# Rebuilding the landmark stage of a four-stage transformer kernel: band matrices by transfer, landmark sums as products, scaling on ScalarE, projections by halves

## The chip, the core and the metric

The kernel runs on one core of one Trainium2 chip. The metric is the device time of one execution in microseconds (us), the median of several executions. TensorE, VectorE (DVE in the rows), ScalarE (ACT), GpSimd (POOL) and SyncE (SP, which issues transfers) run at the same time and wait for each other through semaphores.

## What is computed

The input x is 8 batches of 512 tokens with 256 features. Four layers follow one another: a Nyström attention A, a mixture of experts, an attention B, the experts again. Only attention A and the work ahead of it are touched:

```python
qkv = x @ w_qkv                      # x is layer-normalised; 16 heads of 64
q_l = q.reshape(b, H, M, l, DH).sum(axis=3) / l      # 64 landmarks of 8 tokens each
k_l = k.reshape(b, H, M, l, DH).sum(axis=3) / l
attn1 = softmax(q @ k_l.T); attn2 = softmax(q_l @ k_l.T); attn3 = softmax(q_l @ k.T)
attn2_inv = moore_penrose_inverse(attn2)   # starts from attn2.T / (max col sum * max row sum), over all batches
out = attn1 @ attn2_inv @ (attn3 @ v)
out = out + conv(out)                # 13 taps along the tokens, one set for each head
x = x + out.reshape(...) @ w_fc + b_fc
```

The maximum of the row and column sums is taken over all heads of all batches. So the inverse of the first batch can't begin before `attn2` of the last batch is known, and that is why a stage of its own, `landmarks`, stands ahead of `layer_a`.

## The kernel before

`landmarks` (from L154) works in these steps.

- SP issues the taps and a shifted identity, then the eight batches of x, 512 KB each, then the weights that `layer_a` needs (`la.load`). ACT's queue issues the query and key weights `wqk` (2 MB).
- In a loop of two rounds of four batches, VectorE takes the statistics of a batch (L290, L294), GpSimd makes 1/deviation (L269, L271), VectorE normalises (L300), TensorE transposes in eight products against the identity (L363), and VectorE sums groups of eight tokens out of the bank (L308) into `xsum`.
- When all eight batches are in `xsum`, TensorE makes 16 projections of two products each with 512 columns (L375), eight for `ql`, eight for `kl`; ScalarE scales each out of its bank (L247).
- `build_bands` (L447 to L454) makes the band matrices of the convolution, [128 x 140] for each head, four heads (a quarter) at a time: for each of 13 taps a product with a shifted identity and an addition. VectorE makes two quarters (`BANDS_DVE`) behind its part of the loop, GpSimd one. The fourth is made by GpSimd at the start of `layer_a`.
- Then the softmax of `attn2` over a batch (`sim`, 16 products of 64 columns, L387): VectorE maximum and shift (L325, L327), ScalarE exponential (L252), VectorE sum and reciprocal (L331, L333), GpSimd scaling (L277), TensorE transposition (`aT`, L397), ScalarE copy (L256), VectorE sums of both (L338, L343). At the end the maximum over partitions (L281) and its reciprocal (L350).
- SP stores `ql`, `kl`, `a` and `aT` of every batch to DRAM, 256 KB each, since the loop of `layer_a` loads them batch by batch. It waits for all of these stores at the end of the stage, and a barrier between the stages waits for every engine.

`layer_a` (from L468) begins with a prologue: SP loads the first `a` and `aT`, the value weights into `v_a` (1 MB), and the landmarks of the first batch into the block-diagonal `kl_diag` and `ql_diag`. GpSimd and VectorE zero four block-diagonal tensors. VectorE takes the statistics of batch 0 a second time (L601), GpSimd makes the deviation (L756), VectorE normalises (L613). The value weights are split into two parts, `wv_a_hi` on ScalarE (L872) and `wv_a_lo` on VectorE (L748). GpSimd then builds the fourth quarter of the bands while the loop over the batches runs. A batch begins on TensorE with its transposition (L1004); the products for `u` and `g` (L1012) and the values (L891) come behind. The inverse's steps (L950, L982) are interleaved in an order written out in the code.

The order on every engine is the order of the code; there is no planner. `Fills` gives each use of a PSUM bank its semaphore counts.

## Time and profile before

| | |
|---|---|
| median of 3 executions | 2665.5 us (2656.21 to 2667.6) |
| the profiled execution | 2670.99 us |
| its span in the trace | 2669.2 us |
| TensorE busy | 2247.3 us, 84% of the span |
| VectorE, ScalarE, GpSimd busy | 59%, 38%, 28% |
| mean granted TensorE clock | 0.928 |
| first eight batches' landmarks and the prologue of `layer_a` | 0 to 162.3 us |
| loop of `layer_a` | 162.3 to 1115 us |

The profiled execution takes 1.8 us more than its span. Busy shares are means over stages with different limits. What the change is worth is read from the stretch from 0 to about 290 us, where the stage and the first batch of `layer_a` lie.

### The profile page before, as it was taken

What the parts mean: (1) busy time and instruction counts of PE and PEld (TensorE: products, weight loads), DVE (VectorE), ACT (ScalarE), POOL (GpSimd) and SP (SyncE); (2) the same over time, 40 slices, a digit from 0 to 9 for tenths busy, and PEclk for the clock granted to TensorE, in tenths of its full rate; (3) what the DMA queues carried; (4) which work ended last, traced back from release to release, by engine and by line L of the source; (5) the groups of instructions that cost most, each with busy time, mean ns of one, the idle gap of its engine ahead of it and who ended that gap; (6) DMA issues with size and microseconds to landing.
All of it is one profiled execution on the core that took longest, in us unless ns stands there. A gap on an engine that the chain in (4) does not pass through costs nothing. (4 is left out here: it accounts for less than half of the span.)

```text
span 2669.2 us, 49971 instructions
## 1 busy us (share of the span) xinstructions
PE 2247.3 (84%) x18702; PEld 1776.6 (67%) x18702; DVE 1565.0 (59%) x3407; ACT 1013.9 (38%) x1828; POOL 759.2 (28%) x816
## 2 busy tenths in 40 slices
PE   4469999999999999699859993788888876895998
PEld 2357888788877888577749981445444445774997
DVE  7965547464554646378745653655555526874664
ACT  0223333333333333243424441345454553342553
POOL 4360101010110101136622233333333204662222
PEclk9779999999999999889979996899999998997999
DMA  4320000000000000212345536544444407112553
GB/s 148 99 68 10 10 9 17 2 17 10 9 10 9 11 8 2 78 56 80 127 151 141 140 57 149 91 73 73 74 73 73 73 27 230 40 44 64 139 143 56
DMA packets 152489, 179.60 MB, mean 67 GB/s; under 512 B 48761, under 2 KB 138769, under 8 KB 149137
## 3 DMA queue, kind: packets, MB, share of 16 engines
q1 hardware_dynamic: 137884, 155.67, 21.9%
q0 software_dynamic: 13440, 17.90, 4.1%
q8 instruction: 164, 2.69, 0.4%
q10 hardware_dynamic: 944, 2.88, 0.4%
q14 instruction: 57, 0.46, 0.1%
HBM read 107.66 MB, written 68.75 MB: 66 GB/s over the span
## 5 line engine op out<-in xcount | busy, mean ns | idle before, releaser
L2249 DVE TENSOR_REDUCE b_neg_max<-bank 128x1 f32<-128x512 f32 (+2 forms) x384 | 178.7, 506 | 184.4 <-PE bank L2477 182.1
L2369 ACT ACTIVATE b_probsT<-bank 128x512 f32<-128x512 f32 x320 | 185.9, 604 | 209.8 <-PE bank L2477 198.5
L2008 PE MATMUL bank<-e_hT_hi,k_rwkv 128*128 128x512 f32 x576 | 206.9, 401 | 2.9 <-DVE e_hT_lo L1912 2.9
L1933 DVE TENSOR_TENSOR e_square<-e_relu 128x512 f32<-128x512 f32 x144 | 99.7, 693 | 148.5 <-ACT e_relu L1972 146.1
L774 POOL TENSOR_TENSOR probs<-probs,rcp 128x512 f32<-128x512 f32 x64 | 66.7, 1044 | 382.8 <-DVE rcp L642 382.8
L1972 ACT ACTIVATE e_relu<-bank,k_bias 128x512 f32<-128x512 f32 x144 | 99.1, 688 | 199.4 <-PE bank L2008 199.2
L2021 PE MATMUL bank<-v_rwkv_hi,e_hidden_lo 128*128 (+1 forms) x576 | 162.5, 282 | 0.0
L2021 PE MATMUL bank<-v_rwkv_lo,e_hidden_hi 128*128 (+1 forms) x576 | 162.1, 282 | 0.0
L2021 PE MATMUL bank<-v_rwkv_hi,e_hidden_hi 128*128 (+1 forms) x576 | 161.8, 281 | 0.0
L621 DVE TENSOR_TENSOR conv_lo<-bank,conv_hi 128x512 fp32r<-128x512 f32 x64 | 44.2, 691 | 141.9 <-ACT conv_hi L791 141.9
L2477 PE MATMUL bank<-b_k_stacked,b_q_stacked 96*128 96x512 bf16 (+3 forms) x512 | 126.4, 309 | 0.0
L2008 PEld LDWEIGHTS bank<-e_hT_hi,k_rwkv 128*128 128x128 f32 x576 | 110.0, 191 | 22.3 <-DVE e_hT_lo L1912 3.7
L2477 PE MATMUL bank<-b_q_stacked,b_k_stacked 99*128 99x512 bf16 (+3 forms) x512 | 122.7, 302 | 0.0
L950 PEld LDWEIGHTS bank<-pi_t,wz 64*64 64x64 f32 x3072 | 98.5, 135 | 33.9 <-issue 31.4
L950 PE MATMUL bank<-pi_t,wz 64*64 64x64 f32 x3072 | 111.8, 222 | 5.0 <-DVE pi_t L689 5.0
L2008 PE MATMUL bank<-e_hT_lo,k_rwkv 128*128 128x512 f32 x288 | 114.5, 398 | 0.0
L756 POOL TENSOR_SCALAR a_rstd<-a_mv 128x4 f32<-128x4 f32 x8 | 1.8, 230 | 392.5 <-DVE a_mv L605 381.5
L2021 PEld LDWEIGHTS bank<-v_rwkv_hi,e_hidden_hi 128*128 128x128 f32 x576 | 108.4, 188 | 6.6
L2021 PEld LDWEIGHTS bank<-v_rwkv_lo,e_hidden_hi 128*128 128x128 f32 x576 | 108.6, 188 | 6.0
L1935 DVE TENSOR_TENSOR e_hidden_lo<-e_square,e_hidden_hi 128x512 fp32r<-128x512 f32 x144 | 99.6, 692 | 15.5 <-DVE e_square L1933 0.5
L2021 PEld LDWEIGHTS bank<-v_rwkv_hi,e_hidden_lo 128*128 128x128 f32 x576 | 108.2, 188 | 0.0
L1950 POOL DMA_INDIRECT scratch_x_out<-e_y,e_token x36 | 58.5, 1625 | 172.2 <-DVE e_y L1921 164.0
(358 smaller groups left out, 6431.9 us busy)
## 6 DMA issues: line engine op xcount, KB each, us to landing
k_rwkv<-scratch_k SPq DMA_DIRECT2D x16, 2048.0 KB, 7.4
scratch_b_parts<-b_part SPq DMA_DIRECT2D x96, 128.0 KB, 1.8
b_q_stacked<-scratch_b_parts SPq DMA_DIRECT2D x96, 128.0 KB, 4.5
b_k_stacked<-scratch_b_parts SPq DMA_DIRECT2D x96, 128.0 KB, 4.4
scratch_rows<-f_hq SPq DMA_DIRECT2D x18, 516.0 KB, 8.6
e_rows<-scratch_rows SPq DMA_DIRECT2D x18, 516.0 KB, 8.4
x_tokens<-in_x_dram SPq DMA_DIRECT2D x8, 512.0 KB, 7.7
scratch_x_out<-x_tokens SPq DMA_DIRECT2D x8, 512.0 KB, 3.0
```

Of the source, the lines that this page charges most:

```text
L621: nc.vector.tensor_tensor(lo, fills.data(*name)[:], hi.bitcast(F32), ALU.subtract).then_inc(fills.released(*name), 1)
L774: nc.gpsimd.tensor_tensor(probs, probs, spread(rcp1[:, f], NP), ALU.mult).then_inc(s["probs1_done"], 1)
L950: last = nc.tensor.matmul(data[h, j * M:(j + 1) * M], lhs[h, j], rhs[h, j], start=True, stop=True)
L1933: nc.vector.tensor_tensor(sq[:, q % 2], r[:, q % 2], r[:, q % 2], ALU.mult).then_inc(s["square_done"], 1)
L1935: nc.vector.tensor_tensor(h2[1][:, q % SQ_RING], sq[:, q % 2], h2[0][:, q % SQ_RING].bitcast(F32), ALU.subtract).then_inc(s["hidden_done"], 1)
L1950: nc.gpsimd.indirect_dma_start(x_out[:, :], bass.IndirectOffsetOnAxis(token[:, i % 3, t:t + 1], 0), y[:, i % 2, t, :], None, compute_op=AL ...
L1972: nc.scalar.activation(r[:, q % 2], fl.data("h", q)[:], ACT.Relu, bias=ff.k_bias[i % 2][:, c:c + 1]).then_inc(fl.released("h", q), 1)
L2008: last = nc.tensor.matmul(data[:], ff.k_part(i % 2, a)[:, k, c * P:(c + 1) * P], hT[b][:, i % 2, k], start=n == 0, stop=n == len(steps) - 1)
L2021: last = nc.tensor.matmul(fl.data("e", i, t // 2)[:, t % 2 * C:(t % 2 + 1) * C], h2[a][:, q % SQ_RING, t * P:(t + 1) * P], values[b], star ...
L2249: last = nc.vector.tensor_reduce(neg_max[:, half % 2, t, head + e:head + e + 1], data[:, at:at + (t + 1) * P], AX_X, ALU.max, negate=True)
L2369: nc.scalar.activation(probsT[:, ring, u], fl.data("st", pair, u)[:], ACT.Exp, scale=DB ** -0.5).then_inc(fl.released("st", pair, u), 1)
L2477: last = nc.tensor.matmul(data[:, at:at + size], weights[:, tile:tile + P], moving[:, first:first + size], start=False, stop=True, skip_gr ...
```

## The change

- **Bands.** The band matrices are laid out in the arrays that the kernel is given (`bands`), and come in by one transfer of 1.1 MB with 8960 bytes for each partition. GpSimd adds the centre diagonal in one operation of 2240 columns. `build_bands` is gone from both stages.
- **Landmark sums.** In place of transposing a batch and summing on VectorE, TensorE multiplies the normalised batch with a [128 x 16] matrix of ones (`lm_pool`): eight products of 16 columns (`pool`, L404), and ScalarE copies the sums out of the bank (`take_sums`).
- **Normalising.** ScalarE does it, with scale 1/deviation and bias -mean/deviation; GpSimd makes both in four small steps (`deviation`). Batch 0 is normalised into the tensor that `layer_a` reads, and isn't normalised again there.
- **Halves.** The projections are made for four batches at a time: 8 units of four products with 256 columns for each half. `pool` of batches 4 to 7 stands between those of the first half, `sim` and `aT` of batches 0 to 3 between those of the second.
- **Prologue.** The splitting of the value weights, the zeroing, the multiples of the identity, the fourth quarter and the loads of batch 0 move from `layer_a` into `landmarks`. The value weights land in `v_a`, and `aT` of batches 4 to 7 is later written over them.
- **Row sums.** The sum of the scaled rows is the row sum times its reciprocal, on 8 columns, and not a second reduction over 512.
- The loop of `layer_a` and the three other layers are as before.

```diff
+                load_x(0)
+                sp.dma_start(pool16[:], dram["pool"]).then_inc(consts_loaded, 16)
+                sp.dma_start(la.i64[:], dram["i64"]).then_inc(consts_loaded, 16)
+                for b in range(1, BATCHES_H):
+                    load_x(b)
+                sp.dma_start(wqk[:], dram["w_qkv"][:, 0:2 * INNER].rearrange("(k p) n -> p k n", p=P)).then_inc(w_loaded, 16)
+                for b in range(BATCHES_H, B):
+                    load_x(b)
+                sp.dma_start(wv_raw.rearrange("p (k n) -> p k n", k=CT), dram["w_qkv"][:, 2 * INNER:].rearrange("(k p) n -> p k n", p=P)).then_inc(
+                    wv_loaded, 16)
+                la.load(sp, dram)
                 sp.dma_start(core.ident[:], dram["ident"]).then_inc(core.ident_loaded, 16)
...
+                store_landmarks(0)
+                store_a(0)
+                store_landmarks(1)
+                sp.wait_ge(s["zeroed"], ZEROED)
+                sp.wait_ge(stored_first, 64)
+                la.load_a(sp, 0)
+                la.load_landmarks(sp, 0)
+                for b in range(1, B):
+                    store_a(b)
...
+                def centre(b):
+                    act.wait_ge(s["norm_steps"], (b + 1) * NORM_STEPS)
+                    if b >= 3:
+                        act.wait_ge(*full("pool", b - 2))
+                    for t in range(TT):
+                        nc.scalar.activation(xn_of(b)[:, t, :], cols(x, b * XB + t * C, C), ACT.Identity, bias=nmr[:, b, t:t + 1],
+                                             scale=rstd[:, b, t:t + 1]).then_inc(s["xn_done"], 1)
+                def take_sums(b):
+                    act.wait_ge(*full("pool", b))
+                    nc.scalar.activation(xsum[:, :, b * M:(b + 1) * M], fl.data("pool", b)[:, 0:CT * M].rearrange("p (k m) -> p k m", k=CT),
+                                         ACT.Copy).then_inc(fl.released("pool", b), 1)
...
+                for b in range(BATCHES_H):
+                    centre(b)
+                    if b:
+                        take_sums(b - 1)
+                take_sums(BATCHES_H - 1)
+                for i in range(PROJ):
+                    project(0, i)
+                    if i % 2 == 0:
+                        if i:
+                            take_sums(BATCHES_H + i // 2 - 1)
+                        centre(BATCHES_H + i // 2)
+                take_sums(B - 1)
+                act.wait_ge(wv_loaded, 16)
+                nc.scalar.activation(la.wv[0][:].rearrange("p k n -> p (k n)"), wv_raw, ACT.Copy).then_inc(s["wv_hi"], 1)
+                for i in range(PROJ):
+                    project(1, i)
+                    if i % 2:
+                        exponentials(i // 2)
+                        if i >= 5:
+                            take_turned((i - 5) // 2)
...
-                for n, q in enumerate(range(BANDS_DVE, BANDS_EARLY)):
-                    la.build_bands(nc.gpsimd, pool, n, q, pool_term, pool_signals)
...
+                def deviation(b):
+                    pool.wait_ge(s["mv_done"], (b + 1) * TT)
+                    g.tensor_scalar(var[:, b], mv[:, b, :, 1], EPS, None, ALU.add).then_inc(s["norm_steps"], 1)
+                    g.tensor_tensor(rstd[:, b], var[:, b], core.neg_half[:], ALU.pow).then_inc(s["norm_steps"], 1)
+                    g.tensor_tensor(nm[:, b], mv[:, b, :, 0], rstd[:, b], ALU.mult).then_inc(s["norm_steps"], 1)
+                    g.tensor_scalar(nmr[:, b], nm[:, b], -1.0, None, ALU.mult).then_inc(s["norm_steps"], 1)
+                    deviation(b)
+                pool.wait_ge(consts_loaded, CONSTS)
+                for tile, n in ((la.i7, 7.0), (la.i15, 15.0), (la.i13, 13.0 / 4)):
+                    g.tensor_scalar(tile[:], la.i64[:].unsqueeze(1).to_broadcast([P, GP, M]), n, None, ALU.mult).then_inc(s["eyes_done"], 1)
+                pool.wait_ge(la.loaded, la.loads)
+                g.tensor_tensor(la.band[:], la.band[:], la.centre[:].unsqueeze(1).to_broadcast([P, HA, BAND]), ALU.add).then_inc(s["centred"], 1)
...
-                for q in range(BANDS_DVE):
-                    la.build_bands(nc.vector, dve, q, q, dve_term, dve_signals)
...
+                dve.wait_ge(s["wv_hi"], 1)
+                flat = [w[:].rearrange("p k n -> p (k n)") for w in la.wv]
+                v.tensor_tensor(flat[1], wv_raw, flat[0].bitcast(F32), ALU.subtract).then_inc(s["wv_lo"], 1)
+                for b in range(B + 5):
...
+                        v.tensor_tensor(sums[:, 0, c], row_sum[:, c], row_rcp[:, c], ALU.mult).then_inc(s["rows_summed"], 1)
...
+                def pool(b):
+                    pe.wait_ge(s["xn_done"], (b + 1) * TT)
+                    pe.wait_ge(*free("pool", b))
+                    for t in range(TT):
                         for ct in range(CT):
...
+                            at = ct * M + t * (P // LG)
+                            last = nc.tensor.matmul(fl.data("pool", b)[:, at:at + P // LG], xn_of(b)[:, t, ct * P:(ct + 1) * P], pool16[:],
+                                                    start=True, stop=True)
+                    last.then_inc(fl.filled("pool", b), 1)
+                def proj(half, i):
+                    if i == 0:
+                        for b in range(half * BATCHES_H, (half + 1) * BATCHES_H):
+                            pe.wait_ge(*read("pool", b))
+                        pe.wait_ge(w_loaded, 16)
+                    pe.wait_ge(*free("proj", half, i))
+                    for q in range(2):
+                        n = 2 * i + q
+                        for ct in range(CT):
+                            last = nc.tensor.matmul(fl.data("proj", half, i)[:, q * LANDMARKS_H:(q + 1) * LANDMARKS_H],
+                                                    wqk[:, ct, n * P:(n + 1) * P], xsum[:, ct, half * LANDMARKS_H:(half + 1) * LANDMARKS_H],
+                                                    start=ct == 0, stop=ct == CT - 1)
+                    last.then_inc(fl.filled("proj", half, i), 1)
...
+                pe.wait_ge(consts_loaded, CONSTS)
+                for b in range(BATCHES_H):
+                    pool(b)
+                for i in range(PROJ):
+                    proj(0, i)
+                    if i % 2:
+                        pool(BATCHES_H + i // 2)
+                sim(0)
+                for i in range(PROJ):
+                    proj(1, i)
+                    if i in (4, 6):
+                        turn((i - 4) // 2)
+                    if i in (1, 3, 5):
+                        sim((i + 1) // 2)
+                for b in range(4, B):
+                    sim(b)
+                    turn(b - 2)
+                turn(B - 2)
+                turn(B - 1)
...
-    def build_bands(self, ops, eng, n, q, term, signals):
...
-        for k in range(1, TAPS):
-            eng.wait_ge(band_done, n * BAND_STEPS + k)
-            ops.tensor_tensor(term[:], tap(k), diagonal(k), ALU.mult).then_inc(term_done, 1)
-            eng.wait_ge(term_done, n * (TAPS - 1) + k)
-            ops.tensor_tensor(band, band, term[:], ALU.add).then_inc(band_done, 1)
-        eng.wait_ge(band_done, n * BAND_STEPS + TAPS)
-        ops.tensor_tensor(band, band, diagonal(PAD), ALU.add).then_inc(band_done, 1)
-        eng.wait_ge(band_done, (n + 1) * BAND_STEPS)
...
+                (self.band, dram["bands"].rearrange("p (h n) -> p h n", h=HA)), (self.centre, dram["band_centre"]),
...
-                for diag in (kl_diag, ql_diag):
-                    nc.vector.memset(diag[:], 0.0).then_inc(s["diag_zeroed"], 1)
-                for tile, n in ((i7, 7.0), (i15, 15.0), (i13, 13.0 / 4)):
-                    nc.vector.tensor_scalar(tile[:], la.i64[:].unsqueeze(1).to_broadcast([P, GP, M]), n, None, ALU.mult).then_inc(
-                        s["eyes_done"], 1)
-                dve.wait_ge(s["eyes_done"], 3)
-                statistics(0)
-                normalise(0)
-                dve.wait_ge(s["wv_hi"], 1)
-                flat = [w[:].rearrange("p k n -> p (k n)") for w in wv]
-                nc.vector.tensor_tensor(flat[1], wv_raw, flat[0].bitcast(F32), ALU.subtract).then_inc(s["wv_lo"], 1)
+                dve.sem_inc(s["stats_done"], TT)
+                dve.sem_inc(s["mv_done"], TT)
+                dve.sem_inc(s["xn_done"], TT)
...
-                for diag in (p_diag, avT_diag):
-                    nc.gpsimd.memset(diag[:], 0.0).then_inc(s["wide_zeroed"], 1)
-                inverse_deviation(0)
-                for n, q in enumerate(range(BANDS_EARLY, HA // HB_AT)):
-                    la.build_bands(nc.gpsimd, pool, n, q, band_term, (s["band_done"], s["term_done"]))
+                pool.sem_inc(s["var_done"], 1)
+                pool.sem_inc(s["rstd_done"], 1)
...
+def bands(taps):
+    out = np.zeros((P, HA, BAND), np.float32)
+    for p in range(P):
+        out[p, :, p:p + TAPS] = taps[:, ::-1]
+    return out.reshape(P, HA * BAND)
```

Three places show how this moves instructions. In the rows a line number is that of the kernel concerned, `bank` a PSUM bank, and `[waits ...]` the semaphores that the instruction waits for.

TensorE before, where the loop over the batches ends and the projections begin:

```order
L363 MATMUL bank<-ident,lm_xn 128x128 [waits bank_free7]
L363 MATMUL bank<-ident,lm_xn 128x128 x3
L356 REGISTER_ALU
L356 COMPARE_AND_BRANCH
L375 MATMUL bank<-lm_xsum,wqk 128x512 [waits bank_free5,bank_free6,bank_free4,bank_free7,bank_free3,wqk_loaded,bank_free2,bank_free0,bank_free1]
L375 MATMUL bank<-lm_xsum,wqk 128x512
```

TensorE in the changed kernel, at the beginning of the projections (`lm_pool` is the matrix of ones, `lm_xn` a normalised batch):

```order
L417 MATMUL bank<-lm_xsum,wqk 128x256 [waits bank_free1,wqk_loaded,bank_free0,bank_free2]
L417 MATMUL bank<-lm_xsum,wqk 128x256 x3
L417 MATMUL bank<-lm_xsum,wqk 128x256 [waits bank_free3]
L417 MATMUL bank<-lm_xsum,wqk 128x256 x3
L404 MATMUL bank<-lm_pool,lm_xn 128x16 [waits bank_free0,lm_xn_done]
L404 MATMUL bank<-lm_pool,lm_xn 128x16 x7
L417 MATMUL bank<-lm_xsum,wqk 128x256 [waits bank_free4]
```

The first projection waited for all eight batches; it now waits for four, and the sums of batch 4 stand behind the second unit.

VectorE before, at the end of the second band quarter, where the softmax begins:

```order
L450 TENSOR_TENSOR lm_dve_band_term<-taps,shifted_ident 128x560 [waits lm_dve_band_done]
L452 TENSOR_TENSOR band<-band,lm_dve_band_term 128x560 [waits lm_dve_term_done]
L454 TENSOR_TENSOR band<-band,shifted_ident 128x560 [waits lm_dve_band_done]
L325 TENSOR_REDUCE lm_neg_max<-bank 128x8 [waits bank_full0,lm_dve_band_done]
L327 TENSOR_TENSOR a<-bank,lm_neg_max 128x512 [waits lm_max_done]
L325 TENSOR_REDUCE lm_neg_max<-bank 128x8 [waits bank_full1]
```

VectorE in the changed kernel, between the last statistics and the softmax:

```order
L359 BN_STATS lm_stats<-x_tokens 128x6 [waits x_loaded7]
L359 BN_STATS lm_stats<-x_tokens 128x6 x3
L362 BN_AGGR lm_mv<-lm_stats 128x2 [waits lm_stats_done] x4
L365 TENSOR_TENSOR wv_a_lo<-v_a,wv_a_hi 128x2048 [waits lm_wv_hi]
L370 TENSOR_REDUCE lm_neg_max<-bank 128x8 [waits bank_full5]
L372 TENSOR_TENSOR a<-bank,lm_neg_max 128x512 [waits lm_max_done]
L370 TENSOR_REDUCE lm_neg_max<-bank 128x8 [waits bank_full6]
L372 TENSOR_TENSOR a<-bank,lm_neg_max 128x512 [waits lm_max_done]
L376 TENSOR_REDUCE lm_row_sum<-a 128x8 [waits lm_exp_done]
L378 RECIPROCAL lm_row_rcp<-lm_row_sum 128x8 [waits lm_sum_done]
L380 TENSOR_TENSOR lm_sums<-lm_row_sum,lm_row_rcp 128x8 [waits lm_rcp_done]
```

The softmax stood behind 52 band operations; it now stands behind the lower part of the value weights. The last row is the row sum of the scaled matrix, 8 columns wide.

SP before, at the border of the stages (`scratch_` tensors lie in DRAM; `a_in` and `at` are what the inverse of a batch reads):

```order
L234 DMA scratch_a<-a 128x512 [waits a_done]
L236 DMA scratch_aT<-aT 128x512 [waits bank_free7]
L203 UNCONDITIONAL_BRANCH [waits weights_a_loaded,landmarks_stored]
L559 UNCONDITIONAL_BRANCH [waits barrier_Pool_Activation_PE_DVE_SP_release]
L569 DMA a_in<-scratch_a 128x512
L569 DMA at<-scratch_aT 128x512
L573 DMA v_a<-in_w_qkv_dram 128x2x1024
L564 DMA kl_diag<-scratch_kl 64x8x64 [waits a_diag_zeroed]
```

SP in the changed kernel, where the loads of batch 0 now stand, behind the second half's landmarks:

```order
L227 DMA scratch_ql<-ql 1024x1x64
L227 DMA scratch_kl<-kl 1024x1x64
L503 DMA a_in<-scratch_a 128x512 [waits landmarks_stored_first,lm_zeroed]
L503 DMA at<-scratch_aT 128x512
L498 DMA kl_diag<-scratch_kl 64x8x64 x2
L498 DMA ql_diag<-scratch_ql 64x8x64 x2
L232 DMA scratch_a<-a 128x512 [waits lm_a_done]
L234 DMA scratch_aT<-aT 128x512 [waits bank_free7]
```

The loads for batch 0 stood behind the end of the stage; they now stand in it, ahead of the stores of `a` and `aT` of batches 1 to 7, which have moved behind them and behind the landmarks of the second half.

## Rows read from the trace of the kernel before

**Rows 1.** Windows of the first eight batches and their prologue; columns in the first line.
```profile
core 0: us, PE busy (x) PEld busy (x) DVE busy (x) ACT busy (x) POOL busy (x), PEclk, DMA share, GB/s
0.00:52.60 52.60, 15.52 (x64) 12.55 (x64) 36.93 (x113) 1.28 (x1) 18.41 (x28) 1.00 0.60 187
52.60:82.90 30.30, 29.10 (x64) 12.64 (x64) 29.72 (x19) 9.55 (x16) 28.89 (x19) 1.00 0.00 1
82.90:111.40 28.50, 3.95 (x128) 3.84 (x128) 27.31 (x36) 0.00 (x0) 2.95 (x2) 0.62 0.66 148
111.40:143.20 31.80, 16.22 (x384) 15.38 (x384) 26.76 (x52) 9.14 (x16) 8.74 (x10) 0.71 0.36 134
143.20:162.30 19.10, 1.97 (x32) 1.81 (x32) 9.25 (x18) 2.64 (x3) 8.12 (x9) 0.50 0.39 110
162.30:289.80 127.50, 117.35 (x1224) 99.82 (x1225) 71.39 (x132) 42.06 (x81) 42.17 (x34) 0.93 0.04 10
289.80:998.60 708.80, 674.65 (x7347) 572.53 (x7345) 384.12 (x780) 254.98 (x492) 75.00 (x74) 0.97 0.04 10
```

**Rows 2.** Timeline of the start: start us, length us, engine, line.
```profile
1.44 0.39 SPq L434 DMA_DIRECT2D taps<-in_taps_dram  x1
3.98 15.01 SPq L212 DMA_DIRECT2D x_tokens<-in_x_dram  x8
14.32 1.41 DVE L290 BATCH_NORM_STATS2 lm_stats<-x_tokens 128x6 f32 x4 [14.32 <-DMA x_tokens<-in_x_dram]
15.65 0.41 DVE L294 BATCH_NORM_AGGREGATE lm_mv<-lm_stats 128x2 f32<-128x6 f32 x4
```

**Rows 3.** The projections' matmuls: durations ns min/median/max, first and last start.
```profile
L375 PE MATMUL bank<-lm_xsum,wqk x64: 592/592/1191, 53.0 to 81.5; 128*128 128x512 f32 x64
```

**Rows 4.** Timeline of VectorE at the end of its two band quarters.
```profile
110.61 0.74 DVE L454 TENSOR_TENSOR band<-band,shifted_ident 128x560 f32<-128x560 f32 x1
111.39 0.69 DVE L325 TENSOR_REDUCE lm_neg_max<-bank 128x8 f32<-128x512 f32 x1
```

**Rows 5.** Timeline of the softmax of two batches, the bound, and the next stage's prologue.
```profile
124.81 1.10 PE L387 MATMUL bank<-kl,ql 64*64 64x64 f32 x32
126.83 0.68 DVE L325 TENSOR_REDUCE lm_neg_max<-bank 128x8 f32<-128x512 f32 x1
129.14 1.04 POOL L277 TENSOR_TENSOR a<-a,lm_row_rcp 128x512 f32<-128x512 f32 x1 [2.25 <-DVE lm_row_rcp L333]
130.12 0.68 DVE L325 TENSOR_REDUCE lm_neg_max<-bank 128x8 f32<-128x512 f32 x1
138.88 0.35 DVE L346 TENSOR_REDUCE lm_top<-lm_sums 128x1 f32<-128x64 f32 x2
...
146.77 1.97 PE L950 MATMUL bank<-at 64*64 64x64 f32 x32 [9.29 <-DMA at<-scratch_aT]
151.55 1.91 ACT L872 ACTIVATE wv_a_hi<-v_a 128x2048 fp32r<-128x2048 f32 x1 [13.43 <-DMA v_a<-in_w_qkv_dram]
155.60 0.25 POOL L756 TENSOR_SCALAR a_rstd<-a_mv 128x4 f32<-128x4 f32 x1 [10.59 <-issue]
162.03 2.28 DVE L748 TENSOR_TENSOR wv_a_lo<-v_a,wv_a_hi 128x2048 fp32r<-128x2048 f32 x1
162.34 1.94 PE L1004 MATMUL bank<-ident,a_xn 128*128 128x128 f32 x8 [13.60 <-DVE a_xn L613]
```

**Rows 6.** Groups by form, whole span: xcount, busy us, mean ns, idle before.
```profile
L1647 ACT ACTIVATE f_xn<-x_tokens,f_nmr,f_rstd 128x256 f32<-128x256 f32 x64 | 33.3, 591 | 3.0 <-ACT f_gate L1613 2.6 <-POOL f_nm L1550 0.2
L1549 POOL TENSOR_TENSOR f_rstd<-f_var,neg_half 128x4 f32<-128x4 f32 x16 | 16.8, 1050 | 1.3
```

**Rows 7.** Windows of three stretches in which transfers run; the last column is GB/s.
```profile
15.00:30.00 15.00, 6.50 (x28) 5.42 (x29) 14.65 (x53) 0.00 (x0) 5.33 (x8) 1.00 1.10 348
84.00:104.00 20.00, 3.10 (x107) 2.96 (x102) 19.18 (x25) 0.00 (x0) 1.85 (x2) 0.65 0.95 211
116.00:142.00 26.00, 16.22 (x384) 15.38 (x384) 21.97 (x43) 7.88 (x14) 7.53 (x9) 0.76 0.44 164
```

421 lines of the change are left out of this document (176 added, 245 removed).

## The prediction

> **What bounds the kernel now.** The chain of work that ended last covers the last stage alone, so it doesn't help here; the stages are separated by barriers, and each adds its length. I read the windows first. Up to 162.3 us the kernel prepares landmarks, then eight batches follow [rows 1]. The first batch takes 127.5 us, the next six 708.8 us together, 118.1 us each. GpSimd is busy 42.2 us in the first and 12.5 us in each of the six: the fourth band quarter.
>
> In the preparation no engine is the bound for long. x is requested behind four small loads, beside 2 MB of weights, and VectorE begins at 14.32 us [rows 2]. Until 52.6 us VectorE has most of the work. Then TensorE makes the projections for 29.1 us. Meanwhile VectorE builds bands, and goes on until 111.35 us, when it takes up the softmax, although the projections have been done since 82.9 us; there are 28.5 us in which TensorE works 3.95 us [rows 1, 4]. Softmax and bound take until 143.2 us. The last 19.1 us wait for loads, for GpSimd, and for VectorE, before batch 0 is transposed at 162.34 us [rows 5].
>
> **The change, part by part.** I follow the new order from the start, with durations of the rows.
>
> *To the first projection.* The first load is now x, issued where the taps stood, at 1.4 us. 0.52 MB at 348 GB/s are 1.5 us [rows 7], and I add 3 us for issue and landing, an estimate from two loads of 0.26 MB each at the border, which release TensorE 3.6 us after the stage begins [rows 1, 5]: 5.9 us (at latest 14.3, as now). Statistics 1.41 + 0.41 us [rows 2]; four GpSimd steps, one of 1.05 and three of 0.25, with gaps 2.0 us [rows 5, 6]; four ScalarE operations, 33.3/64 = 0.52 us each, 2.1 us [rows 6]: batch 0 is normalised at 11.8 us. After that the slowest member sets the pace: loads 1.5, VectorE 1.8, GpSimd 2.0, ScalarE 2.1 plus about 0.35 for the copy, so 2.4 us a batch; batch 3 is normalised at 19.0 us. The eight products with 16 columns aren't in the trace. The nearest row is the eight transpositions of the same tiles, 1.94 us [rows 5]. As full products leave two records each (the projections' 32 leave 64, [rows 3]), the bounds are 0.9 and 3.9 us; I take 2.0 at first and 1.4 later. Projections start at 21 us. The 2 MB of weights are there: 4.2 MB at 348 GB/s end near 16 us.
>
> *First half.* A unit has as many columns as one of the 16 old projections, 29.1/16 = 1.8 us [rows 1]. ScalarE normalises batch 4 only behind the scaling of the first unit, and TensorE needs it behind the second, so a turn of two units costs 1.8 + 0.6 (scaling, an estimate from the pace of the projections, which it does not slow) + 0.3 + 2.1 + 1.4 = 6.2 us, of which TensorE waits about 1.2. Four turns: 46 us.
>
> *Second half.* Eight units 14.6 us, four `sim` and two `aT` of 1.1 us each [rows 5], 21.2 us: 67.1 us, scaled at 67.7. The softmax of batches 0 to 3 hides here; so do the lower part of the value weights (2.28 us of VectorE, [rows 5]) and the upper (1.91 us of ScalarE). The bands' 1.1 MB and all the loads are 11.9 MB, 34 us at 348 GB/s: done at 38 us. GpSimd adds the centre before the first scaling near 55 us. If the loads were 15 us late, this addition would hold up the softmax.
>
> *The end on VectorE.* An old batch of softmax takes 130.12 - 126.83 = 3.3 us [rows 5]; a wide sum becomes a narrow one, so 2.8. From `sim` 4 (68.8 us) four of them: 80 us. Exponential, sum, reciprocal, scaling 1.04, `aT`, copy and column sum are 5.9 us more, and from the maxima to the border 143.2 - 138.88 = 4.3 us: 90 us.
>
> *The end on SP.* SP is passed by more than it was. At 67.7 us it issues eight stores with rows of 256 bytes, 2.1 MB; the old ones ran at 211 GB/s [rows 7]: 9.9 us, 1.2 us after issue, until 78.8. The loads of batch 0 are 0.5 MB at 348 and 0.5 MB at 211 GB/s, 4.0 us: 82.8. Only then come 14 stores of 0.26 MB, which used to go out one by one during the softmax. Their rate lies between 211 GB/s and 164/0.44 = 373 [rows 7], 9.8 to 17.4 us; with rows of 2 KB I take 360: 10.2 us, 1.3 more to land: 94.3 us. SP, not VectorE, closes the stage, 48.9 us earlier than now.
>
> *The prologue.* Everything batch 0 needs is loaded. TensorE makes the first step of the inverse, 1.97 us, and transposes about 2.8 us after the border, where it needs 19.1 now [rows 1, 5]: 16.3 us gained.
>
> *Batch 0* loses its extras: no fourth quarter, no splitting of weights, no scaling late in the queue. It becomes like the others, 127.5 - 118.1 = 9.4 us (at least 5, if part of its excess is the slow start of TensorE, at most 11) [rows 1].
>
> Sum: 48.9 + 16.3 + 9.4 = 74.6 us, all on the path, since nothing behind the loop depends on an absolute time. The profiled execution took 2671.0 us; it becomes 2596.4. The median of the runs is 5.5 us below that execution, so I forecast **2591 us**, with 2583 to 2599 for this case. Chance 0.55.
>
> **Rival 1: TensorE stays slow.** The projections' first records took 1191 ns, the later ones 592 [rows 3]; in windows where TensorE works in pieces the granted clock is 0.62 and 0.71 [rows 1], a mix of 1.2 and 2.4 GHz. The changed kernel cuts one run of 29.1 us into units with waits between. If all 16 units ran at the lower level: 16 x 1.8 = 29 us more, 2620; for half of them 2606. Against it: in both halves TensorE waits about 1 us in 6, and batch 0, with shorter pieces, has 0.93. Chance 0.15. The Trainium skill (TensorE: Matmul & The Clock Gate, HAM oscillation — how this bites in real kernels) says that short groups of products with waits for transfers between them keep falling back to half clock; the low windows of this trace agree, and by that rule alone the time would be the 2620 above.
>
> **Rival 2: an engine stands still for its own program.** At the border GpSimd is idle for 10.59 us before L756 and nothing that it waits for is missing ("issue"); it resumes when the transfers have ended [rows 5]. The same beside 34 us of loads, now that the loops are written out, delays the stage by up to 10.6 us: 2602. Against it: none occurred during the loads of before. Chance 0.15. The Trainium skill (Runtime: NRT & Kernel Launch, Instruction fetch mechanics) says that instructions are themselves fetched by transfers, ahead of their use, and that a branch out of the fetched part waits; it would make this idle time a fetch behind data, which no row proves.
>
> **Rival 3: the stores are no bound.** If they run at 373 GB/s and TensorE's small products cost 0.9 us, VectorE's end decides at 86 us: 2582. Chance 0.12.
>
> **Rival 4, the other side: the loop pays.** The loop of `layer_a` is taken back seven times. It begins elsewhere in each engine's program now. Should a standstill of the size of [rows 5], 10.6 us, occur in each of the eight batches, 85 us are lost, more than the 74.6 gained: 2676. It decides from 9.3 us a batch. The six equal batches show none, and transfers take 0.04 there. Chance 0.03, of which 0.02 fall near no change.
>
> **How the numbers follow.** About 0.5% (13 us) is what a measurement of this kernel can tell from no change. Cases 1 and rivals 2 and 3 lie inside 2577 to 2611, rival 1 about half; with a few us for the baseline's own scatter (2656 to 2668) some 0.15 is left out. All but rival 4 are faster by over 50 us: faster 0.97, same 0.02, slower 0.01.
>
> **What will show it.** VectorE starts near 6 us; the first product with 256 columns near 21, `sim` 0 near 46, `sim` 4 near 68; the last engine at the border is SP near 94, the stores of `a` leaving in one dense group after about 83; transposition of batch 0 within 3 us of the border; batches of 118 us, the first too. I am wrong if VectorE still waits long for x, if the units take 3.6 us each, if the border comes after 110, or if later batches are longer.

## The result and the profile after

The changed kernel takes 2599.4 us (median of 4 runs, 2591.3 to 2601.0), the kernel before 2666.6 beside it: ratio 0.975, 95% interval 0.972 to 0.978. 2591 was forecast, 2577 to 2611 as the range. The profiled execution took 2601.0 us with a span of 2599.2, 70.0 us less than that of before, where the forecast had 74.6.

The first view is again the windows, cut at the points that the prediction named [rows 1]:

```profile
core 0: us, PE busy (x) PEld busy (x) DVE busy (x) ACT busy (x) POOL busy (x), PEclk, DMA share, GB/s
0.00:11.50 11.50, 0.00 (x0) 0.01 (x1) 3.81 (x18) 3.36 (x5) 5.84 (x15) 1.00 0.74 258
11.50:26.40 14.90, 14.03 (x65) 13.87 (x65) 9.08 (x47) 7.02 (x16) 9.82 (x23) 1.00 1.04 391
26.40:56.80 30.40, 27.27 (x128) 22.93 (x128) 0.00 (x0) 12.67 (x27) 9.30 (x9) 0.89 0.33 105
56.80:80.90 24.10, 23.19 (x257) 18.94 (x258) 10.62 (x18) 9.16 (x15) 3.12 (x3) 0.93 0.47 110
80.90:102.20 21.30, 11.44 (x320) 10.61 (x320) 15.64 (x35) 6.50 (x12) 5.58 (x6) 0.83 0.95 263
102.20:107.50 5.30, 0.00 (x0) 0.00 (x0) 0.03 (x1) 0.00 (x0) 0.00 (x0) 0.50 0.63 242
107.50:110.30 2.80, 1.88 (x32) 1.82 (x32) 0.35 (x1) 0.47 (x1) 0.00 (x0) 0.50 0.01 3
110.30:226.90 116.60, 110.68 (x1226) 93.90 (x1224) 64.36 (x130) 42.66 (x82) 12.15 (x12) 0.98 0.04 11
...
343.90:462.80 118.90, 113.50 (x1225) 96.19 (x1224) 63.88 (x131) 42.58 (x83) 12.08 (x12) 0.96 0.04 10
462.80:578.70 115.90, 110.57 (x1227) 93.62 (x1224) 63.75 (x131) 42.53 (x83) 12.11 (x12) 0.99 0.04 11
```

The landmark sums of the first four batches end at 26.4 us, the first half of the projections at 56.8, the second at 80.9, VectorE at 102.2, the stage at 107.5; batch 0 is transposed at 110.3. In the 5.3 us from 102.2 to 107.5 no engine works and transfers go on. The timeline of TensorE and of what it waits for at the start, which answers to [rows 2, 3]:

```profile
5.47 1.41 DVE L359 BATCH_NORM_STATS2 lm_stats<-x_tokens 128x6 f32<-128x256 f32 x4 [5.47 <-DMA x_tokens<-in_x_dram]
9.35 2.08 ACT L268 ACTIVATE a_xn<-x_tokens,lm_nmr,lm_rstd 128x256 f32<-128x256 f32 x4 [6.60 <-POOL lm_nmr L336]
11.52 3.57 PE L404 MATMUL bank<-lm_pool,a_xn 128*128 128x16 f32 x16 [11.52 <-ACT a_xn L268]
15.26 10.42 PE L404 MATMUL bank<-lm_pool,lm_xn 128*128 128x16 f32 x48 [0.17 <-ACT lm_xn L268]
26.36 5.59 PE L417 MATMUL bank<-lm_xsum,wqk 128*128 128x256 f32 x16 [0.68 <-ACT lm_xsum L273]
32.75 1.96 PE L404 MATMUL bank<-lm_pool,lm_xn 128*128 128x16 f32 x16 [0.81 <-ACT lm_xn L268]
34.56 3.70 PE L417 MATMUL bank<-lm_xsum,wqk 128*128 128x256 f32 x16
...
41.79 6.40 PE L417 MATMUL bank<-lm_xsum,wqk 128*128 128x256 f32 x16
```

The same 16 records (the products of one batch) take 3.57 us at 11.5 us, 3.5 each in the next three batches, and 1.96 at 32.8; the same two units take 5.59, 3.70 and 6.40 us. The granted clock beside the last of them, and after it:

```profile
42.00:45.00 3.00, 3.00 (x8) 2.37 (x9) 0.00 (x0) 0.00 (x0) 0.60 (x1) 0.50 0.00 0
...
48.00:51.00 3.00, 2.84 (x21) 2.57 (x21) 0.00 (x0) 0.83 (x2) 0.00 (x0) 1.00 0.00 0
```

What closes the stage is in the timelines of SP and VectorE, in SP's waits, and, behind the border, in TensorE's and GpSimd's timelines [rows 5]:

```profile
75.65 0.34 SPq L234 DMA_DIRECT2D scratch_aT<-aT  x1
80.71 0.54 SPq L227 DMA_DIRECT2D scratch_ql<-ql  x1
90.27 0.75 SPq L503 DMA_DIRECT2D a_in<-scratch_a  x1
94.26 0.62 SPq L232 DMA_DIRECT2D scratch_a<-a  x1
102.92 0.59 SPq L234 DMA_DIRECT2D scratch_aT<-v_a  x1
```
```profile
102.07 0.16 DVE L392 RECIPROCAL inv_bound<-lm_bound 128x1 f32<-128x1 f32 x1
```
```profile
SPq L214 <- DMA scratch_aT<-v_a: 3.9, 1, 3.9
```
```profile
108.42 1.98 PE L955 MATMUL bank<-at 64*64 64x64 f32 x32 [10.50 <-PEq L214]
110.33 0.90 PE L1009 MATMUL bank<-ident,a_xn 128*128 128x128 f32 x3
...
112.84 0.41 DVE L626 BATCH_NORM_AGGREGATE a_mv<-a_stats 128x2 f32<-128x6 f32 x4
...
120.37 0.25 POOL L768 TENSOR_SCALAR a_rstd<-a_mv 128x4 f32<-128x4 f32 x1 [18.53 <-issue]
```

From 80.71 us SP has work without a gap: eight stores, six loads, then the 14 stores of `a` and `aT` one behind the other, and 3.9 us of waiting for the last; from 96 to 105 us the transfers move 375 to 408 GB/s. GpSimd again stands still for no reason that the profile knows: `a_mv` is there at 113.25, its next step runs at 120.37, and no transfer is under way.

The account of the two profiled executions: transposition of batch 0 at 110.33 instead of 162.34, 52.0 us; batch 0 116.6 us instead of 127.5, 10.9; batches 1 to 6 695.7 us (226.9 to 922.6) instead of 708.8, 13.1; everything behind the last transposition 1676.6 us (2599.2 - 922.6) instead of 1670.6 (2669.2 - 998.6), -6.0. Together 70.0.

### The profile page after: what moved, and what is told of

Read it like the earlier page. It is cut to its first block and busy times, and to the rows that moved or that the text cites. A ratio compares the mean times of both kernels' runs of the same rounds, so it can differ in the third digit from the quotient of the medians.

```text
span 2599.2 us, 50065 instructions
## 1 busy us (share of the span) xinstructions
PE 2250.4 (87%) x18830; PEld 1789.0 (69%) x18830; DVE 1465.8 (56%) x3290; ACT 1031.3 (40%) x1868; POOL 696.7 (27%) x784
## 5 line engine op out<-in xcount | busy, mean ns | idle before, releaser
L768 POOL TENSOR_SCALAR a_rstd<-a_mv 128x4 f32<-128x4 f32 x7 | 1.6, 231 | 396.1 <-DVE a_mv L626 377.6
L1952 POOL DMA_INDIRECT out_dram<-e_y,e_token x36 | 59.1, 1641 | 171.5 <-DVE e_y L1923 163.2
```

The lines of the kernel that those rows point to most:

```text
L1952: nc.gpsimd.indirect_dma_start(x_out[:, :], bass.IndirectOffsetOnAxis(token[:, i % 3, t:t + 1], 0), y[:, i % 2, t, :], None, compute_op=AL ...
```

## The experiments

The same kernel before took 2667 us beside the changed kernel, and 2678, 2674 and 2668 beside the following three groups, which ran at other times and in part on other chips. So ratios to it, and positions in the traces, are compared.

**1. The bands alone (bands_only).** Made from the kernel before:

```diff
-                la.load_taps(sp, dram)
-                for q in range(BANDS_DVE):
-                    la.build_bands(nc.vector, dve, q, q, dve_term, dve_signals)
...
+                (self.band, dram["bands"]...), (self.centre, dram["band_centre"]),
...
+                nc.gpsimd.tensor_tensor(la.band[:], la.band[:], la.centre[:]..., ALU.add).then_inc(centred, 1)
```

> The kernel before with one part of the change alone: the bands come by transfer (1.1 MB behind x) and GpSimd adds the centre; build_bands is gone from both stages. Theory (the softmax waited for the bands, and batch 0 for their fourth quarter): sim of batch 0 is taken up by VectorE at about 83.5 us instead of 111.4, the stage closes near 116 instead of 143.2, because 16 + 16 stores now stand one behind the other on SP (20 us of landmarks, 12 us of a and aT), the transposition of batch 0 stays 19 us behind the border (its own prologue is left), near 135; batch 0 takes 118 to 122 us. Sum 27 + 5 to 9 = 32 to 36 us, about 2634 against 2667 before, half of the whole change. Rival (the stores decide as they did): if stores of landmarks and of a run at 211 GB/s together, the border comes at 124 and the gain is 24 to 28 us. Rival (the bands cost nothing in batch 0): batch 0 stays at 127 and the gain is 27 us.

Measured: 2639.3 us, ratio 0.985 (0.982 to 0.988), 39 us less than before by the medians. VectorE takes up the softmax at 82.2 us; the border is at 115.9, where SP's next load goes out at 116.03. The prologue is still there:

```profile
119.59 1.97 PE L920 MATMUL bank<-at 64*64 64x64 f32 x32 [11.26 <-DMA at<-scratch_aT]
132.12 1.30 PE L974 MATMUL bank<-ident,a_xn 128*128 128x128 f32 x5 [10.56 <-DVE a_xn L585]
```

Transposition is 30.2 us earlier than before, batch 0 takes 119.3 us, 8.2 less: 38.4 of the 62.9 us that the changed kernel has gained by the end of batch 0. The other 24.5 are the prologue (2.8 us from border to transposition instead of 16.2), 8.4 us of an earlier border, and 2.7 in batch 0. The theory holds; in the trace the gain is 2 us above its upper end, since the prologue shrank too. No kernel takes the landmark sums as products, the scaling on ScalarE or the shorter row sums by itself: that the 8.4 us of the border come from these parts is read from positions and not shown for each; experiment 4 gives the share of the halves.

**2. Is it the clock (warm_lead, warm_all)?** Extra products that nobody reads, in gaps of TensorE:

```diff
+                def busy(products, columns):
+                    for _ in range(products):
+                        nc.tensor.matmul(banks.data[7][:, 0:columns], cols(x, 0, P), cols(x, 0, columns), start=True, stop=True)
+                pe.wait_ge(x_loaded[0], 16)
+                busy(3, 512)
                 pe.wait_ge(consts_loaded, CONSTS)
```

> The changed kernel with three extra products of 512 columns, whose results nobody reads, between the landing of x of batch 0 (5.4 us) and the first product of the landmark sums (11.5 us). sim 4 comes at 74 to 76 us, the border at 101 to 103, the time is 5 to 6 us less, about 2594. Rival (products with 16 columns cost 3.5 us a batch at first for another reason, such as the first use of the code or operands that share a port with the loads): they stay at 3.5 us, and the extra products only delay: the first projection at 26.4 to 28 us, time 2599 to 2601.

Measured: 2600.0 us, ratio 0.973 (0.969 to 0.976), where 2594 was expected. In the timeline of TensorE:

```profile
5.37 5.43 PE L443 MATMUL bank<-x_tokens 128*128 128x512 f32 x6 [5.37 <-DMA x_tokens<-in_x_dram]
11.39 1.93 PE L404 MATMUL bank<-lm_pool,a_xn 128*128 128x16 f32 x16 [0.59 <-issue]
15.11 10.42 PE L404 MATMUL bank<-lm_pool,lm_xn 128*128 128x16 f32 x48 [1.79 <-ACT lm_xn L268]
```
```profile
18.00:21.00 3.00, 3.00 (x16) 3.00 (x15) 2.27 (x11) 2.24 (x5) 0.42 (x2) 0.50 1.11 359
```

The sums of batch 0 fall from 3.57 to 1.93 us. Those of batches 1 to 3 stay at 3.5 each, and here, where the trace has recorded the change, the granted clock beside them is 0.50: the clock is their price. The first projection starts at 26.2, not 21, `sim` 4 comes at 81.3 and the transposition at 110.5, as in the changed kernel. The theory is right on the cause and wrong on the cure.

With products in the later gaps as well (`busy(1, 256)` behind the sums of batches 0 to 2, `busy(2, 256)` ahead of the sums of batches 4 to 7 and of `sim` 0):

> As the run before, and with extra products of 256 columns in the gaps too: one behind the landmark sums of batches 0, 1 and 2, and two ahead of each of the landmark sums of batches 4 to 7 and ahead of sim 0, where TensorE stands still for 1 us. Theory (the waits let the clock fall, and that doubled the units at 42 and 58 us): no unit pair takes over 3.8 us, the granted clock stays 1.00 up to 81 us, turns of the first half take 6.3 us, sim 4 comes at 68 to 71 us and the border near 97 to 100 (SP behind the landmark stores of the second half): 8 to 12 us less, about 2590. Rival (the falls have nothing to do with the waits): the clock still falls once or twice for about 3 to 6 us and sim 4 comes at 74 us or later. Rival (the extra products cost what they save): each is 0.6 us at the higher clock; nine of them lie in gaps of 0.8 to 1.1 us, so at most 3 us are lost.

Measured: 2614.5 us, ratio 0.977 (0.974 to 0.979), where 2590 was expected.

```profile
13.24 0.90 PE L443 MATMUL bank<-x_tokens 128*128 128x256 f32 x2
14.41 3.60 PE L404 MATMUL bank<-lm_pool,lm_xn 128*128 128x16 f32 x16 [0.27 <-ACT lm_xn L268]
...
41.92 3.70 PE L417 MATMUL bank<-lm_xsum,wqk 128*128 128x256 f32 x16
```

All pairs of units but the first now take 3.70 to 3.72 us and the clock stays up from 33 to 66 us. That the filled waits did this is not shown: the changed kernel of experiment 5 with five more stores (shift_border) has the waits, 1.08 us before each sum of batches 5 to 7, and in its profiled execution no pair but the first takes over 3.72 us either:

```profile
33.00:75.00 42.00, 38.76 (x362) 33.04 (x362) 10.62 (x18) 18.15 (x35) 8.06 (x4) 1.00 0.35 88
```

In the sums of batches 1 to 3 of warm_all the clock is down although TensorE waits 0.3 us at most. `sim` 4 comes at 78.6 us and transposition at 107.50, 2.8 us earlier than in the changed kernel. Yet the time is not better: the loop up to the last transposition takes 827.8 us, 15.5 more than in the changed kernel. Experiment 5 shows which batches are longer, not why.

**3. SP's order (order_sp, order_fills).** `ql` of the second half is stored behind its fourth unit, `a` of batches 1 and 2 and `aT` of 0 and 1 beside it, `kl` behind the eighth:

```diff
-                store_a(0)
-                store_landmarks(1)
+                store_plain(0)
...
+                store_rows(1, ((ql, la.ql),))
+                store_plain(1)
+                store_turned(0)
+                store_plain(2)
+                store_turned(1)
...
+                store_rows(1, ((kl, la.kl),))
```

> The changed kernel with another order on SP: the stores of the second half's ql go out when the fourth unit of that half is scaled (69 us), those of its kl after the eighth as now; a of batches 1 and 2 and aT of 0 and 1 go out between them, in the stretch 64 to 81 us in which transfers stood at 0.08. Theory (SP closes the stage because 3.7 MB of stores and 1 MB of loads start only at 80.7 us): 1.05 MB of ql and 1.0 MB of a and aT are moved ahead, 5 + 2.6 us; SP would end near 100, and VectorE's end at 102.2 decides: border 102.3 to 103 instead of 107.5, time about 5 us less, 2594. Rival (VectorE's softmax is itself held by something that SP's end only follows): border stays near 107.

Measured: 2594.4 us, ratio 0.968 (0.966 to 0.971), the lowest of all, though its interval touches that of the changed kernel's second run (experiment 5). The last store is issued at 97.47 instead of 102.92 us, VectorE's bound is done at 101.0, and the next stage begins behind SP's wait of 3.2 us for that store, at about 101.9:

```profile
102.80 1.97 PE L974 MATMUL bank<-at 64*64 64x64 f32 x32 [6.02 <-PEq L214]
104.70 1.84 PE L1028 MATMUL bank<-ident,a_xn 128*128 128x128 f32 x8
```

In the execution of the changed kernel with the same `sim` 4 (79.3 us, here 79.2) the transposition is at 108.9, so the order is worth some 4 us, and SP alone had closed the stage. It still ends last, but by less than 1 us. Now this order together with the extra products of the later gaps:

> The SP order of order_sp (border at 101.7 there) and ten extra products of 256 columns in the gaps of the first half, as in warm_all, without those between batches 0 to 3, which only delayed. If the two add: unit pairs 3.7 us but for the first, sim 4 at 77.5 to 78.5 us instead of 80.9, VectorE's end near 99.5 and the border at 99.5 to 100.5; against the changed kernel 7 to 8 us less, if the loop of batches takes the same time. Rival: the loop takes its clock as it comes (0 to 5 of 7 batches at 119 instead of 116 us), and the sum of the two edits is hidden under up to 15 us of that; then the total may be anything from 8 us less to 7 us more while the border is at 100.

Measured: 2602.8 us, ratio 0.973 (0.970 to 0.975). Transposition at 103.14, the earliest of all: up to there the edits add in the trace. The total is no better than with order_sp alone (the intervals touch): the loop up to the last transposition takes 826.3 us where order_sp has 817.6. The rival of this run, that the loop's scatter hides the sum, holds; it allowed for a wide range.

**4. Without halves (whole_projections, whole_pad32, whole_pad4).** Sums of all batches, then 16 projections of 512 columns, then the softmax:

```diff
-                for i in range(PROJ):
-                    proj(0, i)
-                    if i % 2:
-                        pool(BATCHES_H + i // 2)
-                sim(0)
...
+                for b in range(B):
+                    pool(b)
+                for n in range(2 * NP):
+                    proj(n)
```

> The changed kernel without its halves: landmark sums of all eight batches first, then 16 projections of 512 columns in one piece, then the softmax of all batches. Theory A (the halves gain, because the softmax of batches 0 to 3 lies beside the projections of the second half): landmark sums end at 11.5 + 8 x 3.5 = 40 us at TensorE's lower clock, projections 29.1 + 2.5 us, sim 0 at 71, VectorE then needs 8 x 2.8 + 10.2 = 32.6 us, 104, and SP with 20 us of landmark stores, 4 of loads and 14 stores of a and aT ends at 107 to 109: the border is no later than in the changed kernel (107.5), so the halves gain nothing that lasts, time within 3 us of it. Theory B (the halves gain 5 us or more): the landmark sums at the lower clock cost more, sim 0 only at 75 or later, the border at 112 to 116, time 5 to 9 us longer.

Measured: 2639.2 us, ratio 0.987 (0.984 to 0.989). The stage is as theory A said up to `sim` 0 (71.3 us), and transposition comes at 114.2: the halves gain 4 to 5 us against the 108.9 and 110.3 of the changed kernel. Neither theory foresaw the time: it is 45 us above the changed kernel's in the same group. In the traces 43.7 us stand in the loop (853.2 us up to the last transposition, 809.5 in after_again), whose code is the same; one of its batches, and the timeline of TensorE at the start of another:

```profile
604.10:728.80 124.70, 116.61 (x1227) 98.86 (x1224) 64.01 (x130) 42.69 (x82) 12.11 (x12) 0.92 0.04 10
```
```profile
600.22 0.68 PE L927 MATMUL bank<-at 64*64 64x64 f32 x16 [2.50 <-issue]
603.10 1.12 PE L927 MATMUL bank<-at 64*64 64x64 f32 x16 [2.20 <-issue]
```

Each batch begins with 16 products, 32 records. In the changed kernel they stand behind one standstill of 2.2 to 2.8 us, at the taken branch. Here there is a second one in their middle, 2.1 to 2.5 us, and the clock, down at the start of each batch, stays down longer. In front of the loop TensorE's program has 32 products fewer. Two kernels put that to the test:

```diff
                 pe.wait_ge(consts_loaded, CONSTS)
+                for _ in range(32):
+                    nc.tensor.matmul(banks.data[7][:, 0:P // LG], cols(x, 0, P), pool16[:], start=True, stop=True)
```

> whole_projections with 32 extra products of 16 columns (nobody reads them) ahead of the first landmark sum, where TensorE stands still; they give TensorE's program in front of the loop as many products as the changed kernel has there. In whole_projections every batch took 121.5 to 124.7 us instead of 116 to 119, with a second standstill of 2.1 to 2.2 us in each, behind the first 8 of the 16 products of w0 with which a batch begins. Theory (rival 4 of the prediction, in small: the standstill belongs to the place of the loop in TensorE's program): it is gone, the 16 products run in one piece behind one standstill of 2.2 to 2.7 us, batches take 116 to 120 us, the time falls by 7 x 2.2 + up to 7 x 2.8 us, to 2600 to 2625. Rival (the standstill comes from the other order of work or from the loads): it stays, time 2635 to 2647.

> The same with only 4 extra products. By the theory the point at which TensorE stands still moves by 4 products: behind the first 4 of the 16 products of w0 instead of behind the first 8, standstill again 2.1 to 2.2 us, batches of 121 to 125 us, time about 2640. By the rival it stays behind the first 8.

Measured: 2614.8 us, ratio 0.979 (0.978 to 0.981), with 32, and 2639.4 in one run with 4. With 32 the second standstill is gone, with 4 it has moved forward; the two timelines:

```profile
596.69 1.15 PE L930 MATMUL bank<-at 64*64 64x64 f32 x32 [2.17 <-issue]
```
```profile
600.81 0.46 PE L930 MATMUL bank<-at 64*64 64x64 f32 x7 [2.72 <-issue]
603.49 1.55 PE L930 MATMUL bank<-at 64*64 64x64 f32 x25 [2.22 <-issue]
```

32 extra products cost 7.5 us at the start (transposition at 121.7), and the ratio still falls by 0.007, some 19 us, since the first six batches take 115.3 to 119.4 us instead of 121.5 to 124.7. With 4 all six turns show x7 and x25 in place of x16 and x16. The theory holds: the second standstill belongs to the place of the loop in TensorE's program. The loop is 31.1 us shorter with 32 products (822.1), of which six standstills are 13.3; the rest goes with the clock, and how much of it is the clock's own scatter (experiment 5) is open.

**5. The lengths of the batches (after_again, shift_border).** The changed kernel once more, and with five more stores at the end of the stage:

```diff
+                spare = nc.dram_tensor("scratch_spare", (5, P, NP * M), F32, kind="Internal").ap()
+                for n in range(5):
+                    sp.dma_start(spare[n], a[:, 1]...).then_inc(stored, 16)
```

> The changed kernel itself once more, on the same chip as the three that follow, since the kernel before took 2667 us on one chip and 2678 on another. Expected 2600 to 2612, ratio to before 0.975. In the profile: the border at 107 to 108 us, sim 4 at 80 to 81, and batches of the loop of two lengths, 116 to 117 us where TensorE's granted clock is 0.98 or 0.99 and 119 to 120 where it is 0.96; how many of either is open.

> The changed kernel with five extra stores of 0.26 MB on SP at the end of the landmarks stage, into memory that nothing reads: the border comes 3.3 us later (at 0.65 us a store) and nothing else differs. Theory (which batches fall to the lower clock depends on when they begin, not on their code): the batches keep their two lengths, but other ones than in after are long; the time is not simply 3.3 us more, but between -6 and +15 us of after_again. Rival (the lengths are a property of the chip or of noise): the same batches are long as in after_again and the time is 3.3 us more.

Measured: 2594.3 us, ratio 0.972 (0.968 to 0.975), and 2599.5, ratio 0.972 (0.969 to 0.974). The first lies below the 2600 to 2612 expected, and its border is earlier too (transposition at 108.9, `sim` 4 at 79.3). The seven batches that a transposition bounds in the profiled execution, with those of other kernels, and the medians with their ratios, since the groups had different times before:

| kernel | transposition of batch 0, us | lengths of batches 0 to 6, us | time, us (ratio) |
|---|---|---|---|
| after | 110.3 | 116.6 116.9 118.9 115.9 114.9 115.8 113.2 | 2599.4 (0.975) |
| after_again | 108.9 | 115.9 116.3 116.2 115.8 116.4 116.7 112.1 | 2594.3 (0.972) |
| shift_border | 109.3 | 116.7 119.4 116.1 118.9 114.8 116.0 113.1 | 2599.5 (0.972) |
| order_sp | 104.7 | 116.9 116.2 116.2 119.5 119.0 116.2 113.7 | 2594.4 (0.968) |
| warm_all | 107.5 | 116.9 117.0 119.0 119.4 119.5 119.3 116.7 | 2614.5 (0.977) |
| order_fills | 103.1 | 118.9 119.5 119.3 119.4 116.1 116.4 116.8 | 2602.8 (0.973) |
| before | 162.3 | 127.5 116.7 116.5 119.4 119.6 119.7 116.8 | 2666.6 |

A batch of after_again; then the start of a long batch of the changed kernel (that of 118.9 us) and the stretch from 39 to 48 us behind its start; then the same two stretches of a short batch of order_sp (the first of 116.2 us):

```profile
341.10:457.30 116.20, 110.57 (x1226) 93.85 (x1224) 63.81 (x130) 42.65 (x82) 12.09 (x12) 0.98 0.04 11
```
```profile
340.80:349.80 9.00, 7.02 (x91) 6.79 (x92) 5.74 (x18) 3.33 (x6) 2.66 (x4) 0.81 0.01 4
382.80:391.80 9.00, 9.00 (x54) 7.29 (x54) 2.85 (x6) 3.11 (x8) 1.04 (x1) 0.63 0.01 2
```
```profile
218.60:227.60 9.00, 7.07 (x106) 6.70 (x108) 6.27 (x19) 3.84 (x8) 2.46 (x3) 1.00 0.01 2
260.60:269.60 9.00, 9.00 (x77) 7.26 (x78) 3.18 (x6) 3.11 (x8) 1.04 (x1) 0.81 0.00 0
```

In the table a long batch (118.9 us and more) is one with two falls of the clock: one at its start, and one from about 40 to 48 us behind it, where the inverse's products of 64 columns have run. The second is the longer one: over these 9 us the mean granted clock is 0.63. A short batch has one of the two, or the second only half as long (0.81), or none. Batch 6 is 3 us shorter than the others; where it has both falls it takes 116.7 to 116.8. Which batches are long differs between kernels with equal code there. The shift does not settle why: the changed kernel itself has one long batch in one execution and none in the other, and its `sim` 4 wanders (80.9, 79.3, and 76.3 us in shift_border), which cancels the 3.3 us of the extra stores. The same batches do not stay long, so that rival has fallen; that the moment of a batch's start decides is not shown.

**6. GpSimd's 7 us (probe_reduce, no_reduce).** With a small operation behind the all-reduce, and with a copy in place of it, which leaves out the maximum over the partitions:

```diff
                 g.partition_all_reduce(top_all[:], top[:], P, MAX_ALL).then_inc(s["top_all_done"], 1)
+                g.tensor_scalar(var[:, 0], mv[:, 0, :, 1], EPS, None, ALU.add)
```

> The changed kernel with one small tensor_scalar on GpSimd right behind the partition_all_reduce (its result is not read). In the changed kernel GpSimd's first tensor_scalar of the loop waits 7.1 us after its inputs are there, at a time in which nothing is transferred; before, 7.7 us beside transfers. Theory (the first ordinary operation behind the all-reduce costs GpSimd about 7 us, wherever it stands): the small operation runs at about 109, 7 us behind the all-reduce (101.5), the stage may close 1 to 2 us later for it, and the tensor_scalar of the loop follows its inputs within 0.5 us, near 115 instead of 120.4. Rival (it is the first operation of the next stage's code that is late): the small operation runs at once, at 102, and the one of the loop still waits 7 us.

> The changed kernel with a tensor_scalar in place of the partition_all_reduce, so that each partition keeps its own bound; the maximum over the partitions is left out. Theory (the all-reduce is what costs): no GpSimd operation waits for nothing near the border; the copy follows the maxima within 0.5 us instead of 2.3, inv_bound is there 2 us earlier, near 100, and the tensor_scalar of the loop follows its inputs at once. The border stays at 107, because SP closes the stage; time as in the changed kernel, 2588 to 2600. Rival (the code of the next stage): 7 us before the tensor_scalar of the loop stay.

Measured: 2603.1 and 2595.9 us, one run each. GpSimd's timeline, first with the small operation, then with the copy:

```profile
96.96 0.37 POOL L349 PARTITION_ALL_REDUCE lm_top_all<-lm_top  x1 [5.75 <-issue]
104.74 0.25 POOL L350 TENSOR_SCALAR lm_var<-lm_mv 128x4 f32<-128x4 f32 x1 [7.41 <-issue]
110.80 0.22 POOL L769 TENSOR_SCALAR a_rstd<-a_mv 128x4 f32<-128x4 f32 x1 [5.81 <-DVE a_mv L627]
```
```profile
113.32 0.23 POOL L768 TENSOR_SCALAR a_rstd<-a_mv 128x4 f32<-128x4 f32 x1 [13.59 <-DVE a_mv L626]
```

The standstill goes with the all-reduce: 7.41 us behind it in the first, none in the second, where L768 follows `a_mv` at once (in the first, L769 does too). The rival, that the code of the next stage is late, has fallen.

## Why the forecast was nearly right

- **Start of VectorE** 5.9 forecast, 5.47 measured; batch 0 normalised 11.8 and 11.5: right.
- **Landmark sums, the term that was mis-sized.** "I take 2.0 at first and 1.4 later", between bounds of 0.9 and 3.9. Measured 3.5 us at first and 1.96 later. ScalarE does not set the pace of 2.4 us, TensorE does with 3.5; the first projection is at 26.4 instead of 21. warm_lead shows that the clock is what costs (1.93 us for batch 0, then 3.5 at a granted 0.50). The bound of 3.9 was made of records; I chose the value nearest to a row at the higher clock, and did not ask at which clock TensorE is after 11 us of rest.
- **The turn of 6.2 us, four of them.** At the higher clock it is 6.58 us (32.61 to 39.19 in warm_lead). In the changed kernel the first pair of units takes 5.59 and the third 6.40 instead of 3.70, and one pair in the second half 5.05. `sim` 4 was forecast at 67.7 and comes at 80.9; in the execution without any fall but the first, shift_border, at 76.3. So 8.6 of the 13.2 us are the slow sums, the slow first pair and turns a little too short, and 4.6 are falls of the clock.
- **Rival 1** was the nearest: half of the units at the lower level ("for half of them 2606") would have cost 14.5 us; 3 of 8 pairs were partly there. With the same waits of about 1 us in 6 the clock fell in some executions and not in others: after_again has one such fall between 33 and 76 us, shift_border none. For the landmark sums waits are not the whole of it: there it fell beside gaps of 0.3 us. The Trainium skill (TensorE: Matmul & The Clock Gate, HAM oscillation — how this bites in real kernels) describes waits for transfers that are longer than the groups of products between them; the waits between these units are shorter than the groups, and no run here shows that its rule is what let the clock fall.
- **SP closes the stage:** right, and shown by order_sp. Rival 3 is wrong that the stores are no bound, though they ran at 0.26 MB in about 0.65 us, 400 GB/s, above the 373 that it assumed. The whole 13.2 us by which the border is late (107.5 for 94.3) are those of `sim` 4: from `sim` 4 to the border 26.6 us both forecast and measured. That this agrees to a tenth is in part luck: the eight landmark stores took 9.6 us for 11.1, and the 14 stores with the landing of the last 13.2 for 11.5, of which the landing is 3.9 for 1.3.
- **The prologue:** 2.8 us forecast and measured. **Batch 0:** 118.1 forecast, 116.6 measured, in the range of its gain.
- **Rival 2** named the standstill of GpSimd and said that "it resumes when the transfers have ended". That reading has failed: it stands still as long without any transfer, and goes with the all-reduce (experiment 6). In the changed kernel nobody waits for it.
- **Rival 4** did not come about in the changed kernel, but its mechanism is real: whole_projections has it at 2.1 to 2.5 us a batch, and its loop is 31 us longer than that of whole_pad32, 4.4 us a batch, with the clock behind it. I gave it 0.03 with a price of 10.6 us, taken from GpSimd's standstill, which is another thing.
- **Not in the forecast:** 13.1 us in batches 1 to 6. I carried 118.1 us a batch on, a mean of batches of 116.6 and 119.6. It goes with the clock: in the kernel before four of the six batches have both falls (0.97 as the mean of the six), in the changed kernel one. It varies by execution (the loop up to the last transposition takes 809.5 to 815.1 us in after, after_again and shift_border), and gave back as much as the late border cost. That 2591 and 2599 lie close is in part this offset, and so luck.

What stays open: why the clock falls in some batches and not in others, and the 10 us by which the part behind the loop varies between executions (1669 to 1679 us).

## What to carry to other kernels

Price a new small product on TensorE at the clock that it will meet, not at that of the nearest row: after a rest, and among products of few columns, here that was 1.8 times. When several engines' chains meet at a border, follow the queue of SP as well: here moving four stores of `ql` and some of `a` and `aT` ahead gave 4 us in the trace without taking any work away. And when the time of an untouched loop changes, look at the first rows behind its branch and at the granted clock of each turn before explaining it by the edit.
